# An opening rebuilt: weight products moved to GpSimd and double buffered, the first pair of batches taken through its arithmetic alone

## The reference, cut to what matters

```python
# reaction: du_dt, per batch element, on y = x
lap_x = left + right - 2*y        # along the features, reflected ends
lap_y = up + down - 2*y           # along the sequence, reflected ends
r = zX*lap_x + zY*lap_y + zR*y*(1 - y)
# four Mamba layers on r
for i in range(4):
    n = layer_norm(r, ln_g, ln_b)
    xm, z = split(n @ in_proj_w[i].T)
    xm = silu(depthwise_conv4(xm, conv_w[i]) + conv_b[i])
    dt, Bm, Cm = split(xm @ x_proj_w[i].T, [8, 24])
    dt = softplus(dt @ dt_w[i].T + dt_b[i])
    h = scan(exp(dt*A[i]), dt*Bm*xm)           # 16 states, along the sequence
    y = (sum over states of h*Cm + xm*D_skip[i]) * silu(z)
    r = r + y @ out_proj_w[i].T
```

## Time and profile before

| | us |
|---|---|
| median of 3 runs (1562.08 to 1562.66) | 1562.09 |
| the profiled execution's own time | 1561.56 |
| its span, first to last instruction | 1559.9 |
| busy: PE, DVE, ACT, POOL | 1301.7, 1177.8, 989.1, 1113.3 |

### The profile page before, as it was taken

How to read it: one execution, slowest core, us unless ns; L and a number is a source line. 1 busy time by engine, 2 the same in 40 slices (tenths; PEclk the granted TensorE clock), 3 DMA queues, 4 the chain that set the end, 5 groups by cost and what they waited for, 6 DMA issues and landing times.

```text
span 1559.9 us, 20514 instructions
## 1 busy us (share of the span) xinstructions
PE 1301.7 (83%) x5335; PEld 711.2 (46%) x5336; DVE 1177.8 (76%) x1821; ACT 989.1 (63%) x2316; POOL 1113.3 (71%) x755
## 2 busy tenths in 40 slices
PE   5289889988999899989998769499859898888984
PEld 2033333333333333333333237399735565555653
DVE  5399999999999999999999934555424554555554
ACT  3277788778777877787777533133237766666573
POOL 1099999999999999999999922411248565645561
PEclk9599999999999999999999889599969999999996
DMA  5714644464446444644364134311110000000000
GB/s 167 301 58 179 238 172 148 180 237 163 150 179 244 163 162 149 255 163 182 137 237 170 48 89 162 110 45 47 56 31 14 12 21 15 18 4 15 8 8 8
DMA packets 68066, 185.01 MB, mean 119 GB/s; under 512 B 15464, under 2 KB 50220, under 8 KB 59804
## 3 DMA queue, kind: packets, MB, share of 16 engines
q1 hardware_dynamic: 64700, 177.43, 31.4%
q0 software_dynamic: 3296, 6.76, 1.4%
HBM read 162.56 MB, written 21.60 MB: 118 GB/s over the span
## 4 chain that ended last, share of the span: by engine, by line
PE 28%; DVE 24%; issue 15%; POOL 13%; ACT 12%; DMA 4%; SPq 2%; another core or an unknown queue 1%; DVEq 1%; POOLq 0%; ACTq 0%
DVE h L1416 12%; POOL h L1422 10%; DVE h L1395 6%; ACT banks L1380 5%; PE banks L468 5%; PE banks L926 3%; PE banks L985 3%; PE banks L964 2%; PE banks L477 2%; DMA h<-in_skip 2%; PE banks L1000 2%; PE banks L903 2%; POOL h L1402 2%; PE banks L883 2%; PE banks L866 2%
## 5 line engine op out<-in xcount | busy, mean ns | idle before, releaser
L1422 POOL TENSOR_TENSOR h<-h,Cb 128x1024 f32<-128x1024 f32 x256 | 597.9, 2360 | 11.9 <-DVE h L1416 10.7
L1416 DVE TENSOR_TENSOR_SCAN h<-banks,h 128x1024 f32<-128x1024 f32 x256 | 575.3, 2277 | 6.4 <-ACT banks L1380 2.8
L1433 PE MATMUL banks<-h,ident 128*128 128x512 f32 x1024 | 488.3, 610 | 67.2 <-POOL h L1422 36.8
L1380 ACT ACTIVATE banks<-dt,A_cur 128x255 f32<-128x255 f32 x1024 | 424.7, 461 | 158.9 <-DVE h L1416 156.9
L1433 PEld LDWEIGHTS banks<-h,ident 128*128 128x128 f32 x1024 | 184.9, 191 | 352.7 <-issue 216.6
L1395 DVE TENSOR_TENSOR h<-Bb,banks 128x1024 f32<-128x1024 f32 x176 | 210.1, 1201 | 3.9 <-DMA scrS<-h 3.9
L1402 POOL TENSOR_TENSOR h<-Bb,u 128x1024 f32<-128x1024 f32 x80 | 189.4, 2367 | 29.1 <-DMA scrS<-h 29.1
L956 POOL TENSOR_SCALAR h<-h 128x128 f32<-128x128 f32 (+1 forms) x128 | 101.4, 807 | 102.4 <-DVE h L949 102.4
L1278 PE MATMUL banks<-xn,wF 128*128 128x512 f32 x256 | 119.8, 613 | 30.1 <-ACT xn L1270 24.1
L956 POOL TENSOR_SCALAR Cb<-Cb,h 128x128 f32<-128x128 f32 (+1 forms) x128 | 95.7, 764 | 53.9 <-DVE h L949 53.8
L973 DVE COPY Bb<-banks 128x384 f32<-128x384 f32 x64 | 35.4, 554 | 74.1 <-PE banks L964 71.5
(11 more groups left out here) (242 smaller groups left out, 2000.7 us busy)
## 6 DMA issues: line engine op xcount, KB each, us to landing
Bb<-scrX SPq DMA_DIRECT2D x32, 2048.0 KB, 7.0
Cb<-scrX SPq DMA_DIRECT2D x32, 2048.0 KB, 11.2
by_expert<-zero SPq DMA_DIRECT2D x14, 768.0 KB, 10.2
h<-in_L_ffn_w SPq DMA_DIRECT2D x2, 2048.0 KB, 10.6
scrF<-h SPq DMA_DIRECT2D x4, 681.0 KB, 4.3
wF<-scrF SPq DMA_DIRECT2D x4, 681.0 KB
Cb<-by_expert SPq DMA_DIRECT2D x39, 64.0 KB, 1.8
by_expert<-Cb POOLq DMA_DIRECT2D x39, 64.0 KB, 1.8
```

The costliest lines, as they stand in the source:

```text
L1380: m = e.activation(ps_dA[c % 2][:, g, half, 1:S], dts[q][:, half, i * S + 1:(i + 1) * S], ACT.Exp, scale=A_cur[q][:, s:s + 1])
L1416: e.tensor_tensor_scan(chunk(i, c), ps_dA_flat[c % 2], chunk(i, c), 0.0, ALU.mult, ALU.add).then_inc(sem("scan"), 1)
L1422: e.tensor_tensor(h[i][:, rows(c), :, :], h[i][:, rows(c), :, :], both(Cb[i], c), ALU.mult).then_inc(sem("hC"), 1)
L1433: e.matmul(bank(5), ident[:], h_flat[i][:, s * HALVES * S:(s + 1) * HALVES * S], start=(s == 0), stop=False)
```

## The change

It touches the opening alone, and how the weights of layers 1 to 3 are fetched.

- `bundle` moves from DVE to POOL. Layer 0's products are written straight into `wF` and `wS`, with no way through DRAM. Raw weights have two buffers (`raws`) and so have products (`made`), of which only the products go to `scr`. Weights that need no product (`zxp_w`, `out_w`) are loaded straight from the inputs, so `wF` fills by two or three DMAs and `wS` by one or two.
- All four layers' products are stored before slot 0's `store_xd`: SP waits there for `scr` at 48. Only the products that write `h[1]` still wait for `scr`.
- `reaction` loses two DVE operations: `zR*y` becomes `rate(k)` on POOL, and `zX` goes into ACT's copy of the Laplacian, one operation for each batch element.
- `x` is loaded in two pieces, the first pair's 4 token tiles first. PE interleaves transposes and Laplacians in six PSUM banks. PE's first `center` and `var` stand before the Laplacians of the pairs 2 and 3, and ACT's `A` behind its first `xn`.
- DVE does `reaction(0)` and `reaction(1)`, then the first `norm`. One half of slot 0's `u` moves from POOL to DVE. On ACT `ucopy` and two chunks of `dA` go ahead of the second `square`, `lnv`, `rstd`.

```diff
-            e.dma_start(xtok, x_tok).then_inc(sem("x_in"), 16)
+            e.dma_start(xtok[:, 0:4, :], x_tok[:, 0:4, :]).then_inc(sem("x_in0"), 16)
...
-                e.dma_start(wF[:], layer_of(scrF, L)).then_inc(sem("wF"), 16)
+                if L:
+                    e.dma_start(wF[:, 0:FC_Z], layer_of(scr, L)[:, 0:FC_Z]).then_inc(sem("wF"), 16)
+                e.dma_start(wF[:, FC_Z:FC_END], layer_of(io["zxp_w"], L)).then_inc(sem("wF"), 16)
...
-            e.sem_inc(sem("scr"), 32)
-            prepare(0)
-            e.wait_ge(sem("scr"), 64)
+            raw(0)
             load_front(0)
...
             load_out(0)
-            prepare(1)
-            prepare(2)
+            e.dma_start(A_all[:].rearrange("p l s -> p (l s)"), io["A_log"]).then_inc(sem("alog_in"), 16)
+            raw(1)
+            e.wait_ge(sem("wF"), 48)
+            e.wait_ge(sem("wS"), 32)
+            raw(2)
+            store(1)
+            e.wait_ge(sem("scr"), 16)
+            raw(3)
+            store(2)
+            store(3)
+            e.wait_ge(sem("scr"), 16 * (LAYERS - 1))
             for t in range(SLOTS):
...
-                if t == 0:
-                    prepare(3)
-                    e.wait_ge(sem("scr"), 32 * LAYERS + 32)
...
                 e.wait_ge(sem("res"), NPAIR)
-                e.wait_ge(sem("scr"), 32 * LAYERS + 32)
+                if i:
+                    e.wait_ge(sem("scr"), 16 * (LAYERS - 1))
...
+            def rate(k):
+                bb = slice(2 * k, 2 * k + 2)
+                e.wait_ge(sem("xT"), TURNED[k])
+                e.wait_ge(sem("z_in"), 48)
+                e.tensor_tensor(rise[:, bb, :], ypad[:, bb, 1:S + 1], zb[:, 2, bb].unsqueeze(2).to_broadcast([P, 2, S]),
+                                ALU.mult).then_inc(sem("rise"), 1)
+
+            def bundle(L):
+                r_in, r_cw, r_D = raws[L % 2]
+                e.wait_ge(sem(f"raw{L % 2}"), 48 * (L // 2) + 48)
+                if L == 3:
+                    e.wait_ge(sem("scr"), 16)
+                taps = made[L % 2][:, 0:FC_Z] if L else wF[:, 0:FC_Z]
...
+            rate(0)
+            bundle(0)
+            bundle(1)
+            rate(1)
+            rate(2)
+            bundle(2)
+            rate(3)
+            bundle(3)
+            first(e, POOL, "u:0")
...
-            first(e, PE, "center var conv:0 conv:1 z:0 z:1 xproj dt:0 dt:1 +center +var")
+            first(e, PE, "center var")
+            lap(2)
+            lap(3)
+            first(e, PE, "conv:0 conv:1 z:0 z:1 xproj dt:0 dt:1 +center +var")
...
+            first(e, ACTE, "xm:0 xm:1 zs:0 zs:1 exps xd sp_abs sp_exp sp_ln ucopy:n dA:n0 dA:n1 +square +lnv +rstd")
...
-                du(e.scalar_tensor_tensor(out=g, in0=y, scalar=-1.0, in1=y, op0=ALU.add, op1=ALU.mult))
-                du(e.tensor_tensor(g, g, per_batch(2), ALU.mult))
+                e.wait_ge(sem("rise"), k + 1)
+                du(e.scalar_tensor_tensor(out=g, in0=y, scalar=-1.0, in1=rise[:, bb, :], op0=ALU.add, op1=ALU.mult))
                 du(e.tensor_tensor(g, ly, g, ALU.subtract))
-                e.wait_ge(sem("xT"), 5 + k)
-                du(e.tensor_tensor(lx, lx, per_batch(0), ALU.mult))
+                e.wait_ge(sem("xT"), LAPPED[k])
...
-            reaction(0)
-            bundle(0)
-            e.wait_ge(sem("ln_in"), 32)
-            first(e, DVE, "norm")
-            reaction(1)
-            bundle(1)
-            reaction(2)
-            bundle(2)
-            first(e, DVE, "dt")
-            reaction(3)
-            bundle(3)
+            reaction(0)
+            reaction(1)
+            e.wait_ge(sem("ln_in"), 32)
+            first(e, DVE, "norm")
+            reaction(2)
+            reaction(3)
+            e.wait_ge(sem("xT"), 8)
+            for k in range(2):
+                e.memset(ps_dA[k][:, :, :, 0:1], 0.0).then_inc(sem("dA0"), 1)
+            first(e, DVE, "dt u:1")
```

More of the change, by code:

```diff
@@ L1543, in _ @@
             assert count[0] == CONSTS
[L1544 removed]
+            def rate(k):
[5 more added lines that the diff above has]
+            def bundle(L):
+                r_in, r_cw, r_D = raws[L % 2]
+                e.wait_ge(sem(f"raw{L % 2}"), 48 * (L // 2) + 48)
+                if L == 3:
+                    e.wait_ge(sem("scr"), 16)
+                taps = made[L % 2][:, 0:FC_Z] if L else wF[:, 0:FC_Z]
+                skip = made[L % 2][:, FC_Z:FC_Z + HALVES * P] if L else wS[:, SC_D:SC_OUT]
+                e.tensor_tensor(taps.rearrange("p (k e) -> p k e", k=TAPS), r_in.unsqueeze(1).to_broadcast([P, TAPS, 2 * P]),
+                                r_cw.rearrange("p (k e) -> p k e", k=TAPS), ALU.mult
+                                ).then_inc(sem("bun" if L else "wF"), 1 if L else 16)
+                for half in range(HALVES):
+                    e.tensor_scalar(skip[:, half * P:(half + 1) * P], ident[:], r_D[:, half:half + 1], None, ALU.mult
+                                    ).then_inc(sem("bun" if L else "wS"), 1 if L else 8)
+            rate(0)
[7 more added lines that the diff above has]
+            first(e, POOL, "u:0")
             slots(e, in_order(POOL, POOL_ORDER))
@@ L1579, in _, with turned, lap @@
         def _(e):
-            for k in range(4):
-                e.wait_ge(sem("xT_ps"), k + 1)
-                e.activation(ypad[:, 2 * k:2 * k + 2, 1:S + 1], ps_F[k % 2][:].rearrange("p (b l) -> p b l", b=2),
+            def turned(k):
+                e.wait_ge(sem("xT_ps"), TURNED[k])
+                e.activation(ypad[:, 2 * k:2 * k + 2, 1:S + 1], bank(k).rearrange("p (b l) -> p b l", b=2),
                              ACT.Copy).then_inc(sem("xT"), 1)
-            for k in range(4):
-                e.wait_ge(sem("xT_ps"), 5 + k)
-                e.activation(lapx[:, 2 * k:2 * k + 2, :], ps_F[k % 2][:].rearrange("p (b l) -> p b l", b=2),
-                             ACT.Copy).then_inc(sem("xT"), 1)
+            def lap(k):
+                e.wait_ge(sem("xT_ps"), LAPPED[k])
+                e.wait_ge(sem("z_in"), 48)
+                for b in range(2):
+                    m = e.activation(lapx[:, 2 * k + b, :], bank((4 + k) % 6)[:, b * S:(b + 1) * S], ACT.Identity,
+                                     scale=zb[:, 0, 2 * k + b:2 * k + b + 1])
+                m.then_inc(sem("xT"), 1)
+            e.preload_act_table_set("natural_log_exp_and_others")
+            turned(0)
+            turned(1)
+            lap(0)
+            turned(2)
+            lap(1)
+            turned(3)
+            first(e, ACTE, "square lnv rstd xn")
             e.wait_ge(sem("alog_in"), 16)
@@ L1591, in _ @@
             e.activation(A_all[:], A_all[:], ACT.Copy, scale=-1.0).then_inc(sem("A"), 1)
+            first(e, ACTE, "silus")
+            lap(2)
+            lap(3)
             e.wait_ge(sem("A"), 2)
-            e.preload_act_table_set("natural_log_exp_and_others")
-            first(e, ACTE, "square lnv rstd xn silus xm:0 xm:1 zs:0 zs:1 exps xd sp_abs sp_exp sp_ln +square +lnv +rstd ucopy:n dA:n0 dA:n1")
+            first(e, ACTE, "xm:0 xm:1 zs:0 zs:1 exps xd sp_abs sp_exp sp_ln ucopy:n dA:n0 dA:n1 +square +lnv +rstd")
             slots(e, in_order(ACTE, ACT_ORDER))
```

96 lines of the change are left out of this document (47 added, 49 removed).

## The result

| | before | changed |
|---|---|---|
| median of 4 runs, us | 1562.33 (1562.08 to 1562.66) | 1539.43 (1536.67 to 1544.23) |
| the profiled execution, its span | 1561.56, 1559.9 | 1536.67, 1535.0 |
| first scan product on DVE | 79.25 | 57.06 |

The changed kernel takes 0.9857 of the time before, with an interval of 0.9832 to 0.9881: 22.9 us less. The forecast was 1544.5. The first product was forecast at 61.7 and came at 57.06, and the tail, forecast unchanged, was 3.3 us shorter in the profiled execution. The profiled execution is the fastest of the four: the other three took 2.6 to 7.6 us longer.

A forecast was written before the change was run, and what follows sets the result against it. Slots follow at DVE's pace, so the first scan product, held until the last bundle's store landed, sets the time. Moving it from 79.25 to 61.7 saves 17.5 us: 1544.0 profiled, 1544.5 median, range 1537 to 1552.

The forecast's parts named there:

- The wait for the stores, and `Bb`: Before slot 0: the first product no longer waits for weight stores; these are hidden with 4.7 us to spare.
- The start: Opening: DVE's first reaction near 8.2 us, PE waiting for constants as before, `center` near 16, `rstd` near 21.
- Turns between POOL and DVE: Opening: DVE operations with two SBUF inputs wait for POOL's running operation; POOL's next then waits 0.55 us.
- The norm at 28.4: First norm on DVE, delayed by turns with POOL's weight products and rates to 28.4 us, from 21.74 before.
- An earlier start is worth nothing: Opening: starting DVE's reactions earlier gains nothing, because something else ends later, the second reaction waiting on POOL.
- From the norm to `dt`: Front: convolution 1.5 us after the norm at 29.9, the rest as before, `dt` starting at 49.55 us.
- From `dt` to the product: ACT and DVE before slot 0: from `dt` at 49.55 to the first product at 61.7 us, 4.1 for `square` to `rstd`.
- Slot 0: First slot: same operations, convolution done 10.7 us into it, cost 0; might lose 2 us to a colder start.
- The tail: After the slots: as long as before.
- Rival A: Opening: POOL and DVE hardly disturb each other; norm at 23.6, first product 57.0, time 1539.8 us; chance 0.20.
- Rival C: PE's granted clock stays at 0.50 into the slots, making the kernel slower; 1587 us with one whole slot; chance 0.03.

The follow-up runs named there:

- no_products: Changed kernel with the weight products of layers 1 to 3 replaced by GpSimd memsets that read nothing; median 1529.46 us, ratio to before 0.9845.
- x_whole: Changed kernel with `x` loaded in one piece again; median 1534.41 us, ratio to before 0.9879.
- laps_early: Changed kernel with PE's Laplacians of pairs 2 and 3 ahead of the first `center`; median 1533.96 us, ratio to before 0.9873.
- the repeat: Changed kernel measured once more with no edit; median 1530.83 us, ratio to before 0.9850.
- act_order: Changed kernel with slot 1's `square`, `lnv`, `rstd` back ahead of `ucopy` and two `dA` chunks on ACT; median 1531.58 us, ratio to before 0.9851.
- dve_bundle: Changed kernel with all weight products back on DVE, `rate` staying on POOL; median 1529.47 us, ratio to before 0.9841.
- before_sp: Kernel before with layer 3's weight load and store put ahead of slot 0's `store_xd`, its products ahead of `dt`; median 1541.10 us, ratio 0.9919.

## Why the prediction was right, and where it was off

The frame held: slots of 51.7 us that move as a block, the wait for the stores gone, and the arithmetic of the front as the next bound. The median came 5.1 us below the forecast. In the profiled execution, forecast at 1544.0 and measured at 1536.67, the first product accounts for -4.6 us of the difference, the slots for +0.6 and the tail for -3.3. The steps:

- *The wait for the stores, and `Bb`.* Right. SP was free before `xd` came, with the last weight store issued by 31.6 (26.64 + 5.00), where I had its landing near 39.6. No row shows a wait for `Bb` or `Cb` at slot 0.
- *The start.* DVE began at 8.33, forecast 8.2. It isn't as before, though, that PE waits for the constants: before, its first transposes waited for `x` until 7.25, and now for the last constant until 6.47. `center` was forecast near 16 and `rstd` near 21; they came at 17.99 and 24.21, since the first pair was ready at 17.93 instead of 16.25, and `center` and `var` took 2.07 us each at a granted clock of 0.50, where they took 1.12 before at 1.00. That cost nothing here, as the norm waited for DVE.
- *Turns between POOL and DVE.* Right in kind, for 1024 columns too, as no_products shows by its absence. The Trainium skill's section "Who interferes with whom" in "SBUF — State Buffer" also counts copies that can enter a two-port mode; the small copies of `ypad` agree, with 0.89 us in place of 0.17 (8.53).
- *The norm at 28.4.* It came at 26.07. The start of POOL's first product was put at 12.3 us, from a landing after 4.6 us and a queue ahead; it was 10.31. I had the issue 2 us too late, by 6.7: the second DMA's issue took 0.5 us in place of the 2 us that it took before, and the skip weights were issued at 4.62. This is not shown to be why POOL starts early: in x_whole that issue takes 1.85 us, the skip weights are issued at 5.68, and POOL's first product starts at 10.13 all the same. As I had it, three DVE operations sit behind a whole product, but the second of these falls to the first pair. Counted from POOL's start the first pair took 7.6 us in place of 3.95, and from there to the norm it was 8.1 in place of 12.15. That the two nearly cancel is in part luck, as x_whole shows how much depends on which operation meets which. The diagonals were put at 0.5 each behind DVE's; in turns two of them and two DVE operations fit into 1.8 us. Against that, the copies waited.
- *An earlier start is worth nothing.* Wrong. x_whole shows 4 us for 0.74. I had added POOL's work and DVE's to one chain that no earlier start shortens, but which operation sits behind which decides how much of it is on the path.
- *From the norm to `dt`.* Forecast as before, 19.65 us from the convolution's start to `dt`; it was 17.56. The convolution took 7.14 in place of 9.23 us. I had PE idle there as before; the Laplacians of pairs 2 and 3 fill that place, and with them ahead of `center` (laps_early) it took 10.14. This term was mis-sized by 2.1 us, and in the repeat by 0.4.
- *From `dt` to the product.* 11.9 against 12.15. Right in size. The sum has 4.1 us in it for the `square` to `rstd` that now stand behind `dA`, but doesn't say that the old order would have been faster, by about 3 us as act_order shows.
- *Slot 0.* 51.7 against 51.3; a loss of 0.4, in the bounds.
- *The tail.* Taken as fixed; 3.3 us shorter in the profiled execution. In the twelve experiments it was between 636.7 (x_whole: 1533.0 - 896.35) and 641.1 us (dve_bundle: 1532.4 - 891.26) in kernels that don't differ in it, and 640.0 (1539.8 - 899.82) in before_sp, which is the kernel before but for the place of layer 3's weights. So the 3.3 us can't be put down to the change; what makes the tail vary stays open.

Rival A (no disturbance) gave 57.0 for the first product and 1539.8 for the time, which are the numbers that came, for the wrong reason: the operations did wait, and an earlier start of POOL and a faster clock made up for it. That is luck, and the repeat with its slower convolution has 58.73. Rival C did not occur. The prediction also took 3.1 us as a difference that a measurement tells; the four executions of the changed kernel spread over 7.6.

## What to carry to other kernels

Find the wait that ends last ahead of a periodic stretch, and ask what stands ahead of the load it hangs on in its queue: moving one block of loads, with the arithmetic it waits for, was about half of this gain. Before moving elementwise work to GpSimd, count which VectorE operations with two SBUF inputs, and which small copies, it will run beside; here undoing the move changed nothing that could be measured. And when several engines hand over in turn, look at each engine's order for work that sits ahead of a short chain which others wait for.

## What was not expected of the hardware

- A shift of 0.74 us in VectorE's start (0.92 against GpSimd's) became 4.0 us at the norm, with VectorE never idle in between.
- The same program, started alike, ran the same convolution in 7.14 and in 8.83 us in two executions. The four runs of the changed kernel spread over 7.6 us in the first measurement, where those of before spread over 0.6, and over 4.7 us in the repeat, where those of before spread over 3.6.
- The kernel before took 1562.33 us in the first measurement and 1554.01, 1554.91 and 1553.68 in later ones on three chips. Whether that is the chip isn't shown.
